# A graph-attention kernel: in its first edge walk, the two groups of a pair share one wait ahead of their sixteen gathers

## The chip, the core and the metric

The kernel runs on one core of one Trainium2 chip. The metric is the device time of one execution in microseconds (us), as the median of several runs. The core has TensorE (PE, and PEld for its weight loads), VectorE (DVE), ScalarE (ACT), GpSimd (POOL) and SyncE (SP). Each runs its own instruction stream; they meet only in semaphores. Sixteen DMA engines move data between device memory and the on-chip memory (SBUF).

## What is computed

A network of four layers on 6250 nodes and 100000 edges, 256 features a node, all in float32: graph attention with two heads and then with one, a mixture of experts, a mean over neighbours with a small dense layer, and a second mixture. The change concerns the first attention layer. Its reference, cut to what matters:

```python
def gat_layer(x, W, a_l, a_r, b, src, dst, num_nodes):
    z = (x @ W).reshape(num_nodes, heads, d)
    el = jnp.einsum('nhd,hd->nh', z, a_l)
    er = jnp.einsum('nhd,hd->nh', z, a_r)
    e = el[src] + er[dst]
    e = jnp.where(e > 0, e, NEG_SLOPE * e)
    m = jax.ops.segment_max(e, dst, num_segments=num_nodes)
    ex = jnp.exp(e - m[dst])
    s = jax.ops.segment_sum(ex, dst, num_segments=num_nodes)
    alpha = ex / s[dst]
    msg = z[src] * alpha[:, :, None]
    out = jax.ops.segment_sum(msg, dst, num_segments=num_nodes)
    return out + b[None, :, :]
```

The edges are sorted by `dst`. `src` is random, so the rows `z[src]` have to be gathered.

## The kernel before

The program is a chain of eleven phases (L2456). `walk1` is `edge_walk` with two heads (`H == 2`) and with `nodes`, an object that turns finished nodes into the next layer's rows on the side. `walk2` is the same function with one head. `walk3` is a function of its own, `mean_walk`, with its own gather (L1856).

**Tiles and groups.** A tile is 128 edges and a group eight tiles (1024 edges); there are 98 groups. A group's edges end in a window of 80 consecutive nodes. Two groups make a pair, so the walk has 49 pairs; `Z` holds the gathered rows of four pairs, one buffer `Z[k // 2]` a pair, each for sixteen tiles. The loops are unrolled over eight groups (`UNROLL`), `s` is the number of a group and `k` its place among eight.

**Gathers (L578).** POOL's whole stream is `gather(s, k)`, group after group. It waits for `done8`, which TensorE raises when a group's products are done (`done8` starts at 8, so `s + 1` means that group s-8, the last user of this half of the buffer, is through), and for `idx_ready`, which ScalarE raises when it has copied the group's indices (L596). Then it issues eight indirect DMAs, one for each tile (L583), 128 rows of 1048 bytes each.

**ScalarE** turns logits to weights (`exps`, L606), scales the second head's rows (`scale`, L614), and after a group's products runs `window` (L627): wait for `done8`, copy the next indices into `idx[k]`, copy the window out of PSUM (L633), store it. The order of a pair is: `exps`, two times `scale`, the side work's `head` (L381), `window` of the even group, the side work's `copy_out` (L389), `window` of the odd group.

**TensorE (L736, `pair`)** multiplies one-hot tiles with the gathered rows, in quarters of two tiles a group, and puts the small steps of the attention scores for two pairs ahead between the quarters: `turn_el` (L693, the first that needs the gathered rows; it waits for all sixteen gathers of that pair), `turn_ends` (L699, L700), `turn_ins` (L705, L706) ahead of the odd group's second quarter, and `columns` (L711, L712) behind the odd group. The last tile of a group waits for the window copied before it (L724), whose last node it carries over (L727).

**VectorE (L892, `pair`)** answers each of these steps: logits (L847), one-hot tiles (L803), scans of the turned scores (L817), `carries` (L828) which wait for L700, picks and sums of the target scores (L810, L812), `scan_maxima` (L837) which waits for L706, and then the side work's `scale` (L434).

**SyncE** loads the target scores and resets of three pairs ahead (L538 to L543), and loads and stores the side work's rows (L362, L367).

What orders the work is each engine's written order and these semaphores; nothing else plans it. The lines quoted here are the two waits at stake:

```python
pool.wait_ge(done8, s + 1)
pool.wait_ge(idx_ready, s + 1)
```

Of the kernel before, what the change touches and what calls it, by code (L numbers as in the profile page):

```python
# [446 lines left out]
def edge_walk(nc, keep, dram, name, table, heads, nodes=None):  # L447
# [3 lines left out]
    H = heads  # L451
# [7 lines left out]
    with Phase(nc, name) as ph:  # L459
# [58 lines left out]
        def turns(eng):  # L518
            return eng.value_load(keep["n0tab"][0:1, STEP_TAB:STEP_TAB + 1], min_val=LOOPS, max_val=LONG_LOOPS)
# [56 lines left out]
        @block.gpsimd  # L576
        def _(pool):
            def gather(s, k):  # L578
                pool.wait_ge(done8, s + 1)
                pool.wait_ge(idx_ready, s + 1)  # L580
                pool.sem_inc(pool_tick, 1)
                for t in range(GROUP_TILES):
                    pool.indirect_dma_start(  # L583
                        out=Z[k // 2][:, k % 2 * GROUP_TILES + t, :], out_offset=None, in_=table,
                        in_offset=bass.IndirectOffsetOnAxis(ap=idx[k][:, t:t + 1], axis=0)).then_inc(gathered[k], 16)
            n = turns(pool)
            gather(0, 0)
            gather(1, 1)
            with pool.Fori(0, n) as i:
                for j in range(UNROLL):  # L590
                    gather(i * UNROLL + (j + 2), (j + 2) % UNROLL)
# [1967 lines left out]
```

## Time and profile before

| | |
|---|---|
| median of 3 runs | 5288.94 us (5286.85 to 5299.87) |
| the profiled execution | 5308.62 us, its span 5306.6 us |
| PE busy | 3058.9 us (58%) |
| DVE busy | 1986.9 us (37%) |
| ACT busy | 1502.5 us (28%) |
| POOL busy | 2681.1 us (51%) |
| granted TensorE clock, mean | 0.749 of full speed |
| gathers of the first walk, L583 | 784, from 215.1 to 1475.4 us, median 953 ns |
| gathers of the second walk, L583 | 784, from 1574.8 to 2768.3 us, median 953 ns |

A span is counted from the first to the last instruction. A time on POOL is that of issuing a gather; its data lands later. "Idle before" is the time for which an engine did nothing ahead of an instruction, and "<-" names what ended it: "issue" means that nothing seen in the profile did, "remote" that a semaphore was raised at that time by something that the profile can't match with the end of an instruction. The ends of matmuls are modelled from their starts. Index copies alternate in the first walk: the first of a pair is that of its even group.

### The profile page before, as it was taken

What the parts mean: (1) busy time and instruction counts of PE and PEld (TensorE: products, weight loads), DVE (VectorE), ACT (ScalarE), POOL (GpSimd) and SP (SyncE); (2) the same over time, 40 slices, a digit from 0 to 9 for tenths busy, and PEclk for the clock granted to TensorE, in tenths of its full rate; (3) what the DMA queues carried; (4) which work ended last, traced back from release to release, by engine and by line L of the source; (5) the groups of instructions that cost most, each with busy time, mean ns of one, the idle gap of its engine ahead of it and who ended that gap; (6) DMA issues with size and microseconds to landing.
All of it is one profiled execution on the core that took longest, in us unless ns stands there. A gap on an engine that the chain in (4) does not pass through costs nothing. (4 is left out here: it accounts for less than half of the span.)

```text
span 5306.6 us, 61698 instructions
## 1 busy us (share of the span) xinstructions
PE 3058.9 (58%) x11768; PEld 1883.0 (35%) x11768; DVE 1986.9 (37%) x5614; ACT 1502.5 (28%) x4807; POOL 2681.1 (51%) x2732
## 2 busy tenths in 40 slices
PE   3245555555543455554554489921566666666699
PEld 2123333332321222222223478820333333333466
DVE  4246555555533333333336812242222222223222
ACT  2122232332221222222221023311334444444233
POOL 1366666666626666666652145525566666661121
PEclk9667767777766767677775699965777777777799
DMA  6346666666623433333334266675444444442111
GB/s 151 82 97 104 107 106 109 107 108 104 104 52 96 98 95 99 97 97 98 95 90 135 64 200 220 225 226 153 108 123 120 122 119 122 120 122 65 63 55 51
DMA packets 381422, 598.24 MB, mean 113 GB/s; under 512 B 102442, under 2 KB 272078, under 8 KB 380658
## 3 DMA queue, kind: packets, MB, share of 16 engines
q0 software_dynamic: 136000, 386.29, 32.0%
q1 hardware_dynamic: 209138, 172.22, 12.0%
q10 hardware_dynamic: 36160, 38.56, 2.4%
q14 instruction: 104, 0.85, 0.1%
q8 instruction: 20, 0.33, 0.0%
HBM read 489.46 MB, written 107.34 MB: 112 GB/s over the span
## 5 line engine op out<-in xcount | busy, mean ns | idle before, releaser
L583 POOL DMA_INDIRECT walk_rows<-z_two_heads,walk_idx x784 | 794.7, 1014 | 536.3 <-ACT walk_idx L596 302.5
L583 POOL DMA_INDIRECT walk_rows<-z_one_head,walk_idx x784 | 758.3, 967 | 534.6 <-ACT walk_idx L596 301.9
L1861 POOL DMA_INDIRECT walk_rows<-h,walk_idx x784 | 747.5, 953 | 460.6 <-issue 232.8
L2006 PE MATMUL walk_ps_part<-walk_rows,walk_whot 128*80 128x257 f32 x1568 | 538.3, 479 | 244.1 <-issue 138.2
L730 PE MATMUL walk_ps_part<-walk_rows,walk_hot 128*80 128x258 f32 x1568 | 527.4, 469 | 0.6
L730 PE MATMUL walk_ps_part<-walk_rows,walk_whot 128*80 128x257 f32 x1568 | 519.0, 478 | 0.0
L2006 PEld LDWEIGHTS walk_ps_part<-walk_rows,walk_whot 128*80 128x80 f32 x1568 | 266.5, 186 | 441.4 <-issue 405.9
L596 ACT ACTIVATE walk_idx<-keep_src 128x8 int32 x212 | 44.1, 208 | 1293.5 <-remote 952.1
L730 PEld LDWEIGHTS walk_ps_part<-walk_rows,walk_whot 128*80 128x80 f32 x1568 | 267.9, 186 | 175.9 <-issue 127.1
L730 PEld LDWEIGHTS walk_ps_part<-walk_rows,walk_hot 128*80 128x80 f32 x1568 | 254.7, 180 | 132.2 <-issue 72.8
L812 DVE TENSOR_REDUCE walk_er<-walk_picked 128x8 f32<-128x640 f32 x294 | 241.0, 820 | 29.4 <-issue 7.6
L810 DVE TENSOR_TENSOR walk_picked<-walk_hot,walk_erB 128x640 f32<-128x640 f32 x294 | 241.0, 820 | 22.0 <-issue 3.1
L705 PE MATMUL walk_ps_row_scores<-walk_ones,walk_ends 1*32 1x1 f32 (+1 forms) x196 | 20.4, 171 | 384.2 <-DVEq L832 219.2
L624 ACT ACTIVATE walk_rows<-walk_rows,walk_w 128x129 f32<-128x129 f32 x784 | 235.3, 389 | 5.8
L699 PE MATMUL walk_ps_row_scores<-keep_ident,walk_fmax 32*1 32x32 f32 (+1 forms) x98 | 18.5, 188 | 369.6 <-issue 239.2
L1585 PE MATMUL exp_ps_hid<-exp_hT,exp_w 128*128 128x256 f32 x864 | 220.2, 388 | 8.3 <-DMA exp_b<-in_ffn_b 5.7
L1577 PE MATMUL exp_ps_y<-exp_w,exp_g 128*128 128x256 f32 x864 | 222.6, 380 | 0.0
L2120 DVE TENSOR_TENSOR walk_n_y<-walk_n_h,walk_ps_n_rows 128x256 f32<-128x256 f32 x52 | 21.9, 421 | 522.1 <-DMA walk_n_agg<-agg 459.0
L621 ACT ACTIVATE walk_whot<-walk_hot,walk_w 128x80 f32<-128x80 f32 x784 | 202.9, 347 | 20.5 <-issue 12.8
L1887 ACT ACTIVATE walk_whot<-walk_hot,walk_weight 128x80 f32<-128x80 f32 x784 | 206.8, 349 | 0.0
L828 DVE TENSOR_TENSOR_SCAN walk_ends<-walk_rr,walk_ends,walk_ps_row_scores 1x16 f32<-1x16 f32 x147 | 32.9, 224 | 453.1 <-remote 387.4
L1529 POOL DMA_INDIRECT y_tokens<-exp_y,exp_home x108 | 106.1, 982 | 183.1 <-DVE exp_y L1617 166.6
(368 smaller groups left out, 5189.3 us busy)
## 6 DMA issues: line engine op xcount, KB each, us to landing
exp_w<-in_ffn_W SPq DMA_DIRECT2D x108, 512.0 KB
agg<-walk_window ACTq DMA_DIRECT2D x198, 80.3 KB
walk_rows<-z_two_heads,walk_idx POOLq DMA_INDIRECT x784
walk_rows<-z_one_head,walk_idx POOLq DMA_INDIRECT x784
comb_ya<-y_tokens POOLq DMA_DIRECT2D x28, 448.0 KB
walk_rows<-h,walk_idx POOLq DMA_INDIRECT x784
walk_erB<-er_two_heads SPq DMA_DIRECT2D x104, 80.0 KB
agg<-walk_window ACTq DMA_DIRECT2D x99, 80.6 KB
```

Of the source, the lines that this page charges most:

```text
L583: pool.indirect_dma_start(out=Z[k // 2][:, k % 2 * GROUP_TILES + t, :], out_offset=None, in_=table, in_offset=bass.IndirectOffsetOnAxis(ap ...
L621: last = act.activation(S[k % HOTS][:, t, :], S0[k % HOTS][:, t, :], ACT.Copy, scale=w[:, 0, col:col + 1])
L624: last = act.activation(row, row, ACT.Copy, scale=w[:, 1, col:col + 1])
L730: last = pe.matmul(P[k % 2][0:WIN, 0:AW].rearrange("p (h w) -> p h w", w=HW), hot[:, t, :], rows, start=t == 0, stop=t == GROUP_TILES - 1)
L810: dve.tensor_tensor(picked[:, :, :], S0[k % HOTS][:, :, :], erB[q][:, j, :, h].unsqueeze(1).to_broadcast(wide), ALU.mult)
L812: dve.tensor_reduce(er[:, h, j * GROUP_TILES:(j + 1) * GROUP_TILES], picked[:, :, :], axis=AX.X, op=ALU.add)
L1529: pool.indirect_dma_start(out=dram["ys"], out_offset=bass.IndirectOffsetOnAxis(ap=home[k][:, t:t + 1], axis=0), in_=y[k][:, t, :], in_offs ...
L1577: last = pe.matmul(psY[k][t][:, 0:D], g[k][:, hc, t * 128:(t + 1) * 128], W2[k][:, hc, :], start=hc == 0, stop=hc == HC - 1)
L1585: last = pe.matmul(psH[hc % 2][:, 0:BLOCK], W1[k][:, hf, hc * 128:(hc + 1) * 128], hT[k][:, hf, :], start=hf == 0, stop=hf == HALVES - 1)
L1861: pool.indirect_dma_start(out=Z[k // 2][:, k % 2 * GROUP_TILES + t, :], out_offset=None, in_=table, in_offset=bass.IndirectOffsetOnAxis(ap ...
L1887: last = act.activation(S[k % HOTS][:, t, :], S0[k % HOTS][:, t, :], ACT.Copy, scale=weight[k][:, t:t + 1])
L2006: last = pe.matmul(P[k % 2][0:WIN, 0:HW], S[k % HOTS][:, t, :], Z[k // 2][:, k % 2 * GROUP_TILES + t, :], start=t == 0, stop=t == GROUP_TI ...
```

## The change

For one head nothing changes. For two heads the waits ahead of an odd group's gathers go, and those ahead of an even group's ask for one more: the products of both groups of the pair that used the buffer before, and both lists of indices. The sixteen gathers are then issued in a row.

```diff
         def _(pool):
             def gather(s, k):
-                pool.wait_ge(done8, s + 1)
-                pool.wait_ge(idx_ready, s + 1)
+                if H == 1:
+                    pool.wait_ge(done8, s + 1)
+                    pool.wait_ge(idx_ready, s + 1)
+                elif k % 2 == 0:
+                    pool.wait_ge(done8, s + 2)
+                    pool.wait_ge(idx_ready, s + 2)
                 pool.sem_inc(pool_tick, 1)
                 for t in range(GROUP_TILES):
                     pool.indirect_dma_start(
```

## Rows read from the trace of the kernel before

**Rows 1.** Busy us (and counts) by stretch: PE, PEld, DVE, ACT, POOL, PEclk, DMA share, GB/s

```profile
322.00:1462.00 1140.00, 647.72 (x2465) 359.22 (x2464) 655.29 (x1584) 334.90 (x1234) 713.40 (x704) 0.72 0.63 107
...
3727.00:4804.00 1077.00, 703.07 (x2404) 392.56 (x2405) 264.72 (x880) 452.56 (x1460) 679.33 (x712) 0.75 0.45 121
```

**Rows 2.** The line of the index copies, L596, from 322 to 1462 us

```profile
L596 ACT ACTIVATE walk_idx<-keep_src x89: 208/208/210, 322.7 to 1460.9; 128x8 int32 x89
```

**Rows 3.** The list of waits, 322 to 1462: us in total, times, longest us

```profile
POOL walk_rows L583 <- ACT walk_idx L596: 216.6, 53, 8.3
POOL walk_rows L583 <- issue: 209.1, 647, 4.8
...
DVE walk_gkc L837 <- remote: 226.1, 16, 17.1
...
DVE walk_ends L828 <- remote: 34.1, 7, 8.1
```

**Rows 4.** Timeline, first walk: start, us, engine, line, operation, count [idle <-releaser]

```profile
802.56 0.20 PE L706 MATMUL walk_ps_row_scores<-walk_ones,walk_begins 1*32 1x1 f32 x2
...
805.55 0.66 PE L730 MATMUL walk_ps_part<-walk_rows,walk_hot 128*80 128x258 f32 x2
...
815.14 0.15 DVE L837 COPY walk_gkc<-walk_ps_row_scores 32x2 f32<-32x2 f32 x1 [12.17 <-remote]
...
815.40 0.21 ACT L596 ACTIVATE walk_idx<-keep_src 128x8 int32 x1 [9.78 <-remote]
```

**Rows 5.** Timeline of POOL's gathers, first walk, 792 to 832 us

```profile
792.28 0.95 POOL L583 DMA_INDIRECT walk_rows<-z_two_heads,walk_idx  x1 [2.59 <-ACT walk_idx L596]
...
803.21 0.95 POOL L583 DMA_INDIRECT walk_rows<-z_two_heads,walk_idx  x1 [0.30 <-issue]
...
812.00 0.95 POOL L583 DMA_INDIRECT walk_rows<-z_two_heads,walk_idx  x1 [0.30 <-issue]
816.40 0.95 POOL L583 DMA_INDIRECT walk_rows<-z_two_heads,walk_idx  x1 [3.45 <-ACT walk_idx L596]
...
831.61 1.23 POOL L583 DMA_INDIRECT walk_rows<-z_two_heads,walk_idx  x1 [5.37 <-ACT walk_idx L596]
```

**Rows 6.** Timeline of a long run of gathers, first walk, 986 to 1003 us

```profile
986.01 1.33 POOL L583 DMA_INDIRECT walk_rows<-z_two_heads,walk_idx  x1 [4.70 <-ACT walk_idx L596]
...
1000.44 0.23 DVE L828 TENSOR_TENSOR_SCAN walk_ends<-walk_rr,walk_ends,walk_ps_row_scores 1x16 f32<-1x16 f32 x1
...
1002.36 0.21 ACT L596 ACTIVATE walk_idx<-keep_src 128x8 int32 x1 [1.78 <-issue]
```

**Rows 7.** Timeline after POOL's start at 816.40: TensorE, and ScalarE's index copy

```profile
819.04 0.42 PE L693 MATMUL walk_ps_row_scores<-keep_ident,walk_rows 128*32 128x128 f32 x1
...
827.14 0.23 PE L700 MATMUL walk_ps_row_scores<-keep_ident,walk_bmax 32*1 32x32 f32 x1
...
832.88 0.20 PE L706 MATMUL walk_ps_row_scores<-walk_ones,walk_begins 1*32 1x1 f32 x2
...
835.88 0.66 PE L730 MATMUL walk_ps_part<-walk_rows,walk_hot 128*80 128x258 f32 x2
...
830.61 0.21 ACT L596 ACTIVATE walk_idx<-keep_src 128x8 int32 x1 [1.90 <-PE walk_ps_part L730]
```

**Rows 8.** Timeline of the walk's start: the sixteenth gather, and the first transpose

```profile
234.07 0.95 POOL L583 DMA_INDIRECT walk_rows<-z_two_heads,walk_idx  x1 [0.30 <-issue]
...
236.98 0.37 PE L693 MATMUL walk_ps_row_scores<-keep_ident,walk_rows 128*32 128x128 f32 x1 [71.39 <-DMA walk_rows<-z_two_heads,walk_idx]
```

**Rows 9.** Timeline of POOL in the third walk: first gathers of two runs

```profile
4031.36 0.94 POOL L1861 DMA_INDIRECT walk_rows<-h,walk_idx  x1 [4.22 <-ACT walk_idx L1874]
...
4055.43 0.94 POOL L1861 DMA_INDIRECT walk_rows<-h,walk_idx  x1 [4.21 <-ACT walk_idx L1874]
```

**Rows 10.** Timeline of the first walk's end: last gather, and pair 45's second index copy

```profile
1475.43 0.95 POOL L583 DMA_INDIRECT walk_rows<-z_two_heads,walk_idx  x1 [0.30 <-issue]
...
1480.99 0.21 ACT L596 ACTIVATE walk_idx<-keep_src 128x8 int32 x1 [0.95 <-issue]
```

## The prediction

> **What bounds it now.** I read the busy time by stretch first [rows 1]. From 322 to 1462 us, the steady part of the first walk, 704 gathers run, sixteen for each of 44 pairs, in 1140 us: 25.91 us a pair. POOL is busy for 713.40 us, the largest figure of any engine, yet only 63% of the stretch; TensorE has 647.72 and VectorE 655.29. No engine is full. The index copies give the same period: the second copy of pair 0 at 322.7 and that of pair 44 at 1460.9 are 1138.2 us, or 25.87 us a pair, apart [rows 2].
>
> The list of waits says what lies between the gathers [rows 3]. POOL waits 209.1 us for "issue", the 0.30 us between two gathers, and 216.6 us for `walk_idx`, that is for ScalarE's copy. A pair on POOL is thus 713.40/44 = 16.21 us of gathers, 4.75 us of gaps and 216.6/44 = 4.92 us of waits for indices; together 25.88. The last of the three is the only one that the change touches. The other two make a floor of 20.96 us.
>
> Why is ScalarE late? Look at the timeline of one pair [rows 4]. TensorE's L706 (which announces `ins_turned`) ends at 802.76, but VectorE, which waits for it at L837 and nothing else, starts at 815.14 after 12.17 us idle. The second group's last product ends at 806.21; ScalarE copies the indices at 815.40. Two announcements of TensorE, 3.5 us apart, thus reach their readers 0.3 us apart. POOL's rows stand beside them [rows 5]: its run of sixteen gathers goes from 792.28 to 812.95 and the readers wake 2.2 to 2.5 us after it. So I read: **while POOL issues gathers, TensorE's announcements can be held, and they come free some 2.3 us after POOL falls silent**. In this walk VectorE lost 226.1 us at L837 so, 16 times, and 34.1 us at L828, 7 times [rows 3].
>
> A different row shows that this is not always so. In the run from 986.01 the scan L828, which waits for L700's `ends_turned`, starts at 1000.44 with no idle time before it, and the first group's index copy comes at 1002.36, 16 us into the run [rows 6]. A hold catches some announcements, and those behind it.
>
> **The change, part by part.** The `H == 1` branch is the old code, so the second walk stands, and the third has its own function. In the first walk:
> - The waits of odd k go. Inside a run the next group's first gather (803.21, the ninth from 792.28) follows after the same 0.30 us as any other [rows 5], so the waits cost nothing where they are met, and their going gives nothing: term 0.
> - The waits of even k move to both products and both copies. The first group's eight gathers now start with the second index copy rather than with the first. At pair 20 they start at 831.61, 1.0 us after the first copy at 830.61; they would start 1.0 us after the second, as the gathers at 816.40 follow the copy at 815.40. The eight gathers of the odd group follow them, and so end later by eight gathers, 10 us.
> - Nothing but gathers stands on POOL's queue behind the wait; SyncE's and ScalarE's own DMAs are not moved past anything in program order. The indices of the first group simply lie ready longer.
>
> **Cover of the later gathers.** Pair p+4's gathers start with the end of pair p and are first needed at the transpose of pair p+2 (L693). After a second copy at 815.40 that transpose comes at 819.04 [rows 7], so need lies one period and 2.6 us after the burst's start: 27 us at a period of 24.4. The burst takes 15 x 1.257 + 0.95 = 19.8 us, up to 20.7 as in [rows 5]; landing takes 1.9 us more, by the first sixteen (last issued at 234.07, ends 235.02, transpose at 236.98) [rows 8]. 22.6 against 27: covered by 4 us. If that cover were gone, each us would cost 44.
>
> Here the Trainium skill speaks against the change: "DMA: Bandwidth & Descriptors", Rules for kernel authors, says to issue a DMA early and wait for it late. The change issues half of them late. By that rule alone it gains nothing and, where cover runs out, loses; the rows above say that cover holds.
>
> **The new pair.** After a burst that began at a second copy, TensorE's steps are in the rows already [rows 7], counted from POOL's start at 816.40: L700 (`ends_turned`) ends at 10.97, the first group's index copy comes at 14.2, L706 ends at 16.7, the second group's last product at 20.1. Now the burst has sixteen gathers, so all of these fall into it. If the first two pass and the rest are held, all is flushed at the burst's end, 20.0 to 20.9 us, and POOL starts 3.45 us after its end, as at 816.40 [rows 5]. L837 then runs at the flush again, as at 815.14, so the pattern repeats. One wait a pair: 16.21 + 4.75 + 3.45 = **24.41 us** against 25.88, 1.47 less, times 44 = 64.7 us saved. The run 792.28 to 816.40 is such a period already: 24.12. The third walk, whose POOL code is the old one but which runs in bursts of sixteen by itself, shows 24.07 from 4031.36 to 4055.43, with 4.21 idle [rows 9]; with 4.21 the saving is 31 us.
>
> **The end of the walk** gives a little back. The last burst ended 15.4 us after pair 44's second copy (1460.9 to 1476.38) and pair 45's copy followed at 1480.99, 20.1 us after [rows 10]. New: 1.0 to the start, 20.7 of burst, 2.4 to the flush: 24.1, so 4.0 us lost. Sum: -64.7 + 4.0 = -61 us. The profiled execution took 5308.62 us, 0.37% over the median of 5288.94; the sum gives 5248 against it and **5228 us** against the median, which I forecast. The ends of this term: 24.07 a pair gives -76 (5213), 4.21 idle gives -27 (5262).
>
> **Rivals.** (A) *First group's announcement held as well*, on and off. A hold at 13.6 us stops the window copy (L633), on which the second group's last tile waits. After the flush come 0.6 us of copies, 1.3 of TensorE (an estimate: the last tile's 0.66 [rows 7] and as much for the carry product ahead of it), then 1.2 to POOL: period 20.9 + 2.3 + 3.1 = 26.3, that is 0.4 x 44 + 4 = +22, 5311 if at every pair, 5270 if at half. For: the burst will lie over it, where the eight gathers from 816.40 had ended before it. Against: at 1002.36 it passed deep in a run. 14%.
>
> (B) *Slower: the hold catches `ends_turned`.* Place: L700 at 10.97 of each burst. It decides if L828 waits at most pairs. TensorE then cannot reach the second group's last three quarters: after the flush VectorE's carries take 1.0 (an estimate: four scans of L828's 0.23 [rows 6]), and L706 to the last product 3.5 (832.88 to 836.54 [rows 7]), with 1.2 to POOL: 20.9 + 2.3 + 4.7 + 1.2 = 29.1, or with a burst of 20.7, 28.9. That is +3.0 x 44 + 4 = +136: 5425; at a quarter of the pairs with the rest as forecast, 5278. For: the burst reaches over it for the first time; L828 was held 7 times. Against: 7 of 44 only, and it passed at 1000.44. 20%.
>
> (C) *Nothing changes.* The idle time only moves from before the odd group to before the even one, so that waits a pair stay 4.92: 5289 to 5293. The Trainium skill would have it so: "TensorE: Matmul & The Clock Gate", The cost: per-tile semaphore tail, counts some 26 ns for an increment on a matmul, and with no holds POOL's quiet has nothing to free. The trace disagrees (12 us at L837), so 8%.
>
> Forecast 58%.
>
> **Numbers.** 0.3% (16 us) is about what a measurement of this kernel can tell from no change. Faster: forecast, plus part of A and B's mild form, 0.64. Same: C and the middle of A, 0.14. Slower: 0.22. The range starts below the -76 end at 5205 and reaches over A at 5311 to 5325, leaving most of B out.
>
> **To check in the new trace.** Runs of sixteen on POOL throughout the walk, each after 3.4 to 4.2 us idle; the period by index copies near 24.4; POOL's wait for `walk_idx` near 44 rather than 53 times and 150 us rather than 216.6; TensorE's L693 not waiting for a gather; the second walk unchanged. Wrong if L828 waits about 10 us at most pairs (B), if POOL's idle stays at 4.9 (C), or if L693 waits for a DMA.

## The result, and the profile after

The changed kernel took 5334.24 us (median of 10 runs, 5310.56 to 5347.6) where the kernel before took 5295.1 (10 runs) beside it: ratio 1.0065, 95% interval 1.0047 to 1.0083. It is slower, by 0.65%; the forecast of 5228 us was wrong. The profiled execution took 5336.71 us, 28.1 more than that of before. Lines behind L578 have moved by 4 (L596 is L600 now, L837 is L841).

The busy time by stretch, the first walk's steady part and the third walk's:

```profile
322.00:1462.00 1140.00, 697.39 (x2400) 372.04 (x2401) 633.47 (x1534) 325.92 (x1194) 682.43 (x685) 0.70 0.59 104
3727.00:4804.00 1077.00, 680.94 (x2328) 380.83 (x2327) 258.89 (x860) 443.22 (x1427) 672.02 (x706) 0.75 0.45 119
```

Against [rows 1] 685 gathers fit into the stretch and no longer 704. TensorE's granted clock is 0.70, not 0.72; it has more busy time and fewer instructions. The index copies, from pair 0's second to pair 44's:

```profile
L600 ACT ACTIVATE walk_idx<-keep_src x89: 208/208/211, 315.9 to 1487.2; 128x8 int32 x89
```

They are 1171.3 us apart, 44 pairs, 26.62 a pair against 25.87 [rows 2]. So the balance is: pair 0 done 6.8 us earlier (315.9 against 322.7), 44 pairs 33.1 us longer, and the walk's end, from pair 44's copy to pair 45's at 1511.9, 24.7 against 20.1 [rows 10], 4.6 longer. That is +30.9, and the second walk's first gather starts at 1605.58, 30.8 after before's 1574.82. What follows gives some of it back, with unchanged code: the second walk's last gather starts 25.3 us after before's (2793.6 against 2768.3), the third walk's first 27.6 (3653.2 against 3625.6). The whole loss is in the first walk.

The list of waits, 322 to 1462 us (us in total, times, longest):

```profile
ACT walk_idx L600 <- remote: 320.2, 42, 14.8
DVE walk_gkc L841 <- remote: 274.0, 38, 11.1
POOL walk_rows L587 <- ACT walk_idx L600: 241.0, 41, 14.5
POOL walk_rows L587 <- issue: 216.2, 644, 6.9
...
DVE walk_ends L832 <- remote: 14.3, 2, 8.6
...
PE walk_ps_row_scores L697 <- DMA walk_rows<-z_two_heads,walk_idx: 10.1, 8, 3.8
```

Against [rows 3] POOL waits for indices fewer times (41, not 53) but longer (241.0 us, not 216.6), where 150 was forecast. L828's successor L832 was held twice: rival B did not come. L697 hardly waits for a gather: the cover held. What grew is L841's wait, 38 times instead of 16. The list of before has one row more that the prediction did not use, the wait of the index copies themselves:

```profile
ACT walk_idx L596 <- remote: 365.7, 37, 13.6
```

Its total is no smaller than the 320.2 us of after; what changed is which group's copy waits. Of the copies of pairs 1 to 44 in before, the first group's waited for a remote step 3 times, all the others were the second group's. In after the first group's waited so 31 times.

Three runs of sixteen gathers follow, by POOL's timeline (all other gathers between these rows have 0.30 us before them):

```profile
638.48 0.95 POOL L587 DMA_INDIRECT walk_rows<-z_two_heads,walk_idx  x1 [4.69 <-ACT walk_idx L600]
...
657.87 0.95 POOL L587 DMA_INDIRECT walk_rows<-z_two_heads,walk_idx  x1 [0.30 <-issue]
665.96 0.95 POOL L587 DMA_INDIRECT walk_rows<-z_two_heads,walk_idx  x1 [7.14 <-ACT walk_idx L600]
...
690.18 0.95 POOL L587 DMA_INDIRECT walk_rows<-z_two_heads,walk_idx  x1 [3.83 <-ACT walk_idx L600]
...
717.90 0.95 POOL L587 DMA_INDIRECT walk_rows<-z_two_heads,walk_idx  x1 [7.65 <-ACT walk_idx L600]
```

and ScalarE's index copies, first and second group of each pair:

```profile
661.69 0.21 ACT L600 ACTIVATE walk_idx<-keep_src 128x8 int32 x1 [11.38 <-remote]
...
664.95 0.21 ACT L600 ACTIVATE walk_idx<-keep_src 128x8 int32 x1 [0.95 <-issue]
...
676.81 0.21 ACT L600 ACTIVATE walk_idx<-keep_src 128x8 int32 x1 [2.03 <-PE walk_ps_part L734]
...
689.18 0.21 ACT L600 ACTIVATE walk_idx<-keep_src 128x8 int32 x1 [1.30 <-remote]
```

The second pair (start 665.96) comes nearest to the forecast's: the first group's copy passes 10.9 us into the run, the second comes 2.8 us after the run's end (686.36), POOL starts again after 3.83 us, and the period is 24.22 us, where 24.41 was forecast. The first pair (638.48) is rival A: nothing reaches ScalarE until 661.69, 2.9 us after the run's end. Its period is 27.48, and that of the third pair (690.18), held as well, 27.72 (to the next start at 717.90). TensorE's timeline says that the first group's products had long been done:

```profile
648.65 0.18 PE L704 MATMUL walk_ps_row_scores<-keep_ident,walk_bmax 32*1 32x32 f32 x1
...
650.76 1.15 PE L734 MATMUL walk_ps_part<-walk_rows,walk_hot 128*80 128x258 f32 x2
...
673.11 0.23 PE L704 MATMUL walk_ps_row_scores<-keep_ident,walk_bmax 32*1 32x32 f32 x1
...
675.30 1.15 PE L734 MATMUL walk_ps_part<-walk_rows,walk_hot 128*80 128x258 f32 x2
```

The last product ends at 651.91, 13.4 us into its run, and is read 9.8 us later; in the next run it ends at 676.45, 10.5 us in, and is read 0.4 us later. Sorted over the walk by whether ScalarE's first copy comes before or after the end of POOL's run, 24 pairs pass with a mean of 25.4 us and 20 are held with a mean of 28.1; (24 x 25.4 + 20 x 28.1)/44 = 26.6. "Pass" is not "on time": at 11 of the 24 the copy waited 3.7 to 9.7 us for a remote step and then came inside the run.

The two kinds often alternate. In the rows above, TensorE's steps have caught up after the held pair before the next run starts, so the next pair's steps come early in the run (L704 ends 7.4 us in) and pass. After the passed pair, L716 is done only behind the start (690.99 against 690.18), L704 ends 10.4 us in, and the announcement is held again. Over the walk this is a tendency and no rule: where L704 ends less than 9 us into the run, 1 of 12 pairs is held, elsewhere 19 of 32; a held pair follows a held one 7 times.

### The profile page after: what moved, and what is told of

Read it like the earlier page. It is cut to its first block and busy times, and to the rows that moved or that the text cites. A ratio compares the mean times of both kernels' runs of the same rounds, so it can differ in the third digit from the quotient of the medians.

```text
span 5334.8 us, 61650 instructions
## 1 busy us (share of the span) xinstructions
PE 3155.4 (59%) x11768; PEld 1921.4 (36%) x11768; DVE 1981.8 (37%) x5614; ACT 1504.5 (28%) x4807; POOL 2673.0 (50%) x2732
## 5 line engine op out<-in xcount | busy, mean ns | idle before, releaser
L587 POOL DMA_INDIRECT walk_rows<-z_two_heads,walk_idx x784 | 780.6, 996 | 579.1 <-ACT walk_idx L600 332.9
L2010 PE MATMUL walk_ps_part<-walk_rows,walk_whot 128*80 128x257 f32 x1568 | 532.2, 475 | 218.2 <-issue 117.4
L734 PE MATMUL walk_ps_part<-walk_rows,walk_hot 128*80 128x258 f32 x1568 | 573.8, 502 | 0.9 <-issue 0.4
L734 PE MATMUL walk_ps_part<-walk_rows,walk_whot 128*80 128x257 f32 x1568 | 539.2, 492 | 1.5 <-issue 1.2
L600 ACT ACTIVATE walk_idx<-keep_src 128x8 int32 x212 | 44.1, 208 | 1224.4 <-remote 982.7
L734 PEld LDWEIGHTS walk_ps_part<-walk_rows,walk_hot 128*80 128x80 f32 x1568 | 277.3, 195 | 147.2 <-issue 97.7
L715 PE MATMUL walk_ps_cols<-walk_ends,walk_ones 1*128 1x4 f32 (+1 forms) x196 | 47.5, 310 | 367.5 <-DVEq L847 209.1
L814 DVE TENSOR_TENSOR walk_picked<-walk_hot,walk_erB 128x640 f32<-128x640 f32 x294 | 241.1, 820 | 31.4 <-issue 14.2
L841 DVE COPY walk_gkc<-walk_ps_row_scores 32x2 f32<-32x2 f32 (+1 forms) x98 | 14.5, 148 | 614.0 <-remote 541.1
L2124 DVE TENSOR_TENSOR walk_n_y<-walk_n_h,walk_ps_n_rows 128x256 f32<-128x256 f32 x52 | 21.9, 421 | 524.4 <-DMA walk_n_agg<-agg 409.0
```

Of the source, the lines that this page charges most:

```text
L587: pool.indirect_dma_start(out=Z[k // 2][:, k % 2 * GROUP_TILES + t, :], out_offset=None, in_=table, in_offset=bass.IndirectOffsetOnAxis(ap ...
L734: last = pe.matmul(P[k % 2][0:WIN, 0:AW].rearrange("p (h w) -> p h w", w=HW), hot[:, t, :], rows, start=t == 0, stop=t == GROUP_TILES - 1)
L814: dve.tensor_tensor(picked[:, :, :], S0[k % HOTS][:, :, :], erB[q][:, j, :, h].unsqueeze(1).to_broadcast(wide), ALU.mult)
L2010: last = pe.matmul(P[k % 2][0:WIN, 0:HW], S[k % HOTS][:, t, :], Z[k // 2][:, k % 2 * GROUP_TILES + t, :], start=t == 0, stop=t == GROUP_TI ...
```

## The experiments

Five batches, each with the kernel before beside it; runs of one batch are compared only within it. The code below is cut to the edit; `...` marks what is left out. What the kernel before took matters: 5302.88, 5259.63 and 5256.03 us in the first three, 4666.18 and 4664.2 in the last two.

**The first group's announcement made earlier** (on the changed kernel and on before):

```
                 products(s, 2 * m, 2)
+                if H == 2:
+                    products(s, 2 * m, 3)
                 if turn is not None:
                     turn_ends(p + 2)
-                products(s, 2 * m, 3)
+                if H == 1:
+                    products(s, 2 * m, 3)
```

> The changed kernel, with the even group's last quarter of products put ahead of turn_ends on TensorE (first walk only), so that its done8 comes some 5 us earlier in POOL's run of sixteen. Theory H (TensorE's announcements are held while POOL issues; the even group's at 13.6 us into the run is what the change lost): it passes at most pairs, POOL's idle time falls from 5.9 to 3.5-4 us, the pair from 26.6 to 24.4-25 us, the kernel from 5334 to 5240-5265. Rival L (the loss is that half of the gathers start 10 us later, whatever the order on TensorE): 5334, pair 26.6.

> The kernel before with the same edit on TensorE alone. Theory H: the even group's indices are copied earlier, the two runs of eight merge into one of sixteen more often, pair 24.4-25.4 us, kernel 5230-5275. Rival L: no difference, 5295.

`q3_after` took 5351.67 us, 1.0107 of before (1.0089 to 1.0125): slower, where 5240 to 5265 was expected. `q3_before` took 5281.92, 0.9959 (0.9944 to 0.9974): a gain, just short of the expected one. The waits of `q3_after`, 322 to 1462 us:

```profile
POOL walk_rows L587 <- ACT walk_idx L600: 261.5, 43, 11.0
...
DVE walk_ends L835 <- remote: 157.9, 20, 11.6
DVE walk_gkc L844 <- remote: 152.4, 32, 10.3
ACT walk_idx L600 <- remote: 133.1, 24, 11.6
```

The index copy is held much less (133.1 us against 320.2), as wanted, but `ends_turned`, which now comes after it, is held in its place: 157.9 us against 14.3. With the order of the two announcements turned round, the hold went from one to the other, so it isn't bound to one of them.

**Less to gather.** `half_after` issues four of a group's eight gathers in the first walk (the other tiles are zeros); `narrow_after` issues all, each with 131 of a row's 262 numbers (the others are zeros).

```
# half_after (LOADED is 4 with two heads)
-                for t in range(GROUP_TILES):
+                for t in range(LOADED):
# narrow_after (ROW is 131 with two heads)
-                        out=Z[...][:, ..., :], ..., in_=table,
+                        out=Z[...][:, ..., 0:ROW], ..., in_=table.rearrange("n (h w) -> (n h) w", w=ROW),
```

> The changed kernel with four of a group's eight gathers in the first walk (the other rows of the buffer are zeroed once; every other instruction stays). Theory H: POOL's run is 10 us, nearly all announcements fall behind it, and the pair takes what TensorE and VectorE need of each other, 19.5-21 us: kernel 5050-5110. Rival C (the engines' own chain needs 26 us a pair and POOL is a bystander): 5320-5340.

> The changed kernel with all sixteen gathers of a pair but half the bytes in each (131 of 262 elements a row, first walk only; the other half of the buffer is zeroed once). Theory H with POOL's issuing as the cause of the holds: period stays 26-27 us, kernel 5320-5340. Rival D (the traffic of the gathers on the DMA engines holds the announcements): holds shrink, period 20-24 us, kernel 5060-5220.

`half_after` took 4925.6 us (before 5302.88), less than the 5050 to 5110 expected, and `narrow_after` 5329.76, as expected if POOL's issuing is the cause. Each ran once. `narrow_after`'s waits are those of the changed kernel:

```profile
ACT walk_idx L603 <- remote: 315.5, 37, 14.8
DVE walk_gkc L847 <- remote: 267.9, 39, 11.0
```

Half the bytes a gather change nothing. Half the instructions change much. The first walk of `half_after` ends before 1200 us, so its stretch is 322 to 1100 us, which holds 84 index copies:

```profile
ACT walk_idx L603 <- remote: 43.2, 12, 4.4
```

The changed kernel's L600 waits 211.0 us, 28 times, in the same stretch, and the old L841, which waits 180.9 us there, does not wait for a remote step at all. Both kernels move about half the bytes; only the one that issues half the gathers, in runs of eight, loses most of the holds. The holds go with POOL's issuing, not with the traffic that it starts.

**SyncE's part.** While announcements are held, some of SyncE's steps are slow too. A row SPq is one of them. The step that issues L368's DMA takes 0.70 us in the held run above, and about as long at the median of the stretch (ns: shortest, median, longest):

```profile
643.52 0.70 SPq L368 DMA_DIRECT2D er_one_head<-walk_n_z  x1
...
L368 SPq DMA_DIRECT2D er_one_head<-walk_n_z x42: 4/699/728, 347.3 to 1456.1; - x42
```

So a theory S was tried: SyncE's steps beside the gathers hold the announcements. First its six loads of a pair in the first walk were given to ScalarE (`act_*`, behind its second window copy), left out (`quiet_*`), or made to wait until POOL had issued a run's last gather (`gate_*`):

```
# quiet (with two heads)
-                    load(p + AHEAD, (m + AHEAD) % INS)
+                        sp.wait_ge(inputs_used4, p + (AHEAD + 1))
+                        sp.sem_inc(inputs[(m + AHEAD) % INS], LOADS)
# gate: POOL raises `silent` behind each odd group's gathers
+                    if H == 2:
+                        sp.wait_ge(silent, p + 3)
+                        ...
                     load(p + AHEAD, (m + AHEAD) % INS)
```

> The changed kernel, with the six loads of a pair (target scores and resets of four pairs ahead) issued by ScalarE behind its second window instead of by SyncE, in the first walk. Theory S (in a run of gathers each of SyncE's steps takes 0.7 us instead of 0.04, and while it steps so, TensorE's announcements are held; a SyncE that waits holds none): with some 40 steps fewer a pair the even group's announcement passes, POOL's idle time falls to 3.5-4 us, the pair to 24-25 us and the kernel to 5220-5270. Rival P (POOL's issuing alone holds TensorE, whoever else is at work): 5320-5350, and more if ScalarE's own steps slow down.

> The kernel before with the same move of the loads from SyncE to ScalarE. Theory S: L837's holds (226 us in the steady part) shrink by more than half and the kernel is 5150-5250. Rival P: 5280-5310.

> The changed kernel with SyncE's six loads of a pair left out of the first walk's loop (the scores and resets of the first four pairs are used again and again; SyncE only raises the semaphore). Theory S: as act_after or a little faster, 5200-5260. Rival P: 5320-5340.

> The changed kernel, with SyncE's six loads of a pair held back until POOL has issued the last gather of a run, so that most of SyncE's steps fall into POOL's silence. Theory S (TensorE's announcements are held while SyncE steps at 0.7 us a step beside the gathers): most holds in the run go, the first group's index copy passes at two pairs in three or more, period 24.5 to 25.5, time 0.975 to 0.990 of before. Rival P (POOL's issuing alone holds them, SyncE is a bystander): holds stay as they are, 1.003 to 1.010. The node loads and stores of SyncE are not gated, so part of the holds can stay under S as well.

> The same gate on the kernel before. Theory S: fewer of the 12 us waits at L837, period 24.6 to 25.4, time 0.980 to 0.993 of before. Rival P: 0.998 to 1.003.

> The kernel before with the gate and with the last quarter of the first group's products ahead of the transposes of the ends. If the two gains add, 0.976 to 0.989 of before under theory S; under rival P the quarter's gain alone, 0.994 to 0.998.

`act_after` took 5358.07 us, 1.0201 of before (1.0181 to 1.022), `act_before` 5461.05, 1.0397 (1.0364 to 1.043); both are far above theory S's range, and the first is what rival P allows if ScalarE's steps slow down. No index copy waited for a remote step in either, but in `act_after` the old L841 still did (141.2 us, 29 times). ScalarE, behind its DMAs, was late for its own work: its first step of a pair's weights (`exps`) waited, for nothing that another engine did,

```profile
ACT walk_ps_work L614 <- issue: 365.5, 42, 15.8
```

against 94.3 us in the changed kernel, and 487.2 us in `act_before`. POOL stood still longer with it (670 gathers in the stretch, and 629), so these runs can't say whether the copies were on time because SyncE had fewer steps or because the pairs were stretched.

`quiet_after` can say it in part: SyncE has the same steps left in it, and ScalarE none more. It took 5247.37 us in its one run, 0.998 of before's 5259.63, which is in theory S's range, but its waits are not what theory S needs:

```profile
DVE walk_gkc L845 <- remote: 336.9, 44, 9.9
ACT walk_idx L604 <- remote: 265.2, 45, 10.9
```

The loads gone, the holds are still there. At 10 pairs of 44, instead of 20, the first group's copy came only after the run's end, and a pair took 25.3 us in the mean. So SyncE's loads are not what holds announcements, though they may lengthen a hold.

`gate_after` took 1.0072 of before (1.0057 to 1.0087), `gate_before` 1.0004 (0.9992 to 1.0015), `gate_q3_before` 0.9966 (0.9951 to 0.9981). All three are in rival P's ranges, and the gated kernel's index copies are held as long as before:

```profile
ACT walk_idx L608 <- remote: 307.9, 43, 14.3
```

But the gate did not do what it was meant to. By the traces 170 of the 255 load DMAs of SyncE start inside POOL's runs in the changed kernel, and 165 of 264 in `gate_after`; before has 165 of 264, and `gate_before` 185 of 270. Hardly a step was moved into silence, so these runs test neither theory. The quarter's gain of `q3_before` came again (0.9966 beside 0.9959).

**The run split in two**, so that the announcement falls into silence:

```
                 elif k % 2 == 0:
                     pool.wait_ge(done8, s + 2)
                     pool.wait_ge(idx_ready, s + 2)
+                else:
+                    pool.wait_ge(done8, s + 2)
```

> The changed kernel with one more wait: an odd group's gathers also wait for the first products of the next pair. Eight gathers start with a pair, then POOL is silent until the first group's announcement is in, then the other eight follow: the same gathers, the odd ones later still. Theory A (the loss comes from the first group's announcement, due 13.6 us into a run of sixteen, being held): it falls into silence here, so its index copy comes at about 14 to 15 us after POOL's start at nearly every pair, and the loss goes: period 25.2 to 26.1, time 0.985 to 1.000 of before. Rival, the late gathers cost by themselves (transposes or scans wait for them): later gathers cost more, the time is 1.007 or above of before and L697 waits for a gather.

5258.51 us, 1.0003 of before (0.9992 to 1.0014): the loss of the change alone (1.0065 in its own batch) is gone, but not in the way expected, as the waits show:

```profile
PE walk_ps_row_scores L699 <- DMA walk_rows<-z_two_heads,walk_idx: 419.9, 37, 15.2
...
POOL walk_rows L589 <- PE walk_ps_part L736: 164.1, 48, 6.5
...
DVE walk_ends L834 <- remote: 100.4, 25, 5.1
...
ACT walk_idx L602 <- remote: 78.1, 15, 9.5
```

The holds at the index copy shrank (78.1 us against 320.2) and so did all at the old L841; in their place TensorE's transposes wait 419.9 us for gathers, which now come half a pair later still. The odd gathers run together with the next even ones, in runs of sixteen again. Both effects, less hold and less cover, lie in this run, and it prices neither. The time lies between the two ranges.

**The hold's price alone.** In the changed kernel the second group's last tile waits for the first group's window copy, and ScalarE's second index copy comes behind both. `loose_*` cuts that; what a first group carries into the second is left out.

```
-                        pe.wait_ge(win_ready2, s + 2)
+                        alone = H == 2 and k % 2 == 1
+                        if not alone:
+                            pe.wait_ge(win_ready2, s + 2)
                         ...
-                            pe.matmul(..., wsb[1 - k % 2][:, cols], ...)
+                            pe.matmul(..., (nil if alone else wsb[1 - k % 2])[:, cols], ...)
# ScalarE, behind an even group's window copy; the odd group's own wait and index copy go
+                if H == 2 and k % 2 == 0:
+                    act.wait_ge(done8, s + (UNROLL + 2))
+                    copy_idx(second, k + 1)
```

> In the changed kernel the held announcement of the first group costs because the second group's last tile (by the carry product) and ScalarE's second index copy queue up behind it. Here the second group's carry product reads a tile of zeros instead of the first group's window and does not wait for it, and ScalarE copies the second group's indices straight behind the first window copy. What a first group carries into the second is left out, so those rows of the output differ. Theory A: holds stay where they are but cost nothing, the second index copy comes under 1 us behind the first after a run's end, the period is 24.2 to 25.2 at every pair, 0.98 to 0.99 of the kernel before, and the gap to loose_before is gone (0.985 to 1.000). Rival (late gathers, or something else that the change brings): the period stays near 26 and the gap to loose_before stays at 1.005 or more.

> The same edit on the kernel before. Its holds fall on L706's announcement, which this edit does not touch, so it gains what ScalarE's earlier second copy gives, some 1 us at pairs without a hold: 0.985 to 0.998 of before.

> The changed kernel of quiet_after again, timed: SyncE's six loads of a pair are left out and their semaphore is raised at once (pairs then use the input values that the first loads brought, so the output differs). If the loads themselves (their steps, or their transfers) hold announcements in the changed kernel above all, this is 0.990 to 1.000 of the kernel before, and the gap to quiet_before is under 1.003. If they are a bystander, the gap stays at 1.005 or more.

> The same edit on the kernel before: SyncE's six loads of a pair left out. By either theory 0.985 to 1.000 of the kernel before.

Here the ground moved. The kernel before, unchanged, took 4666.18 us (33 runs), 11 to 12% less than in the batches so far, and the four others the same within 0.2%: `loose_after` 1.0016 (1.0007 to 1.0025), `loose_before` 0.9999 (0.999 to 1.0008), `quiet_after3` 1.0002 (0.9993 to 1.0012), `quiet_before` 0.9993 (0.9983 to 1.0002). The expectations for holds could not be tested, because there were next to none (one wait of 2.1 us in `loose_after`, none in the two `quiet` kernels). The same two kernels ran once more, with the changed kernel itself.

> The changed kernel itself, beside the kernel before and the two loose kernels. Where TensorE's announcements are held during runs of gathers (before near 5260 to 5300 us): 1.004 to 1.009 of before by theory A. Where none is held (before near 4666 us, POOL issuing without a pause in the first walk): no hold to price, only the later gathers are left, 1.000 to 1.004.

> loose_after once more, since its first runs fell where nothing was held. Where announcements are held again, theory A: the second index copy comes under 1 us behind the first after a run's end, period 24.2 to 25.2, 0.98 to 0.99 of before and no gap to loose_before (0.985 to 1.000). Rival: period near 26, a gap of 1.005 or more. Where nothing is held: 1.001 to 1.003, as the first time.

> loose_before once more. Where announcements are held: 0.985 to 0.998 of before. Where nothing is held: 0.999 to 1.001.

Again before took 4664.2 us (29 runs). **The changed kernel took 4667.19: 1.0005 (0.9996 to 1.0015)**, no difference. `loose_after2` took 1.0018 (1.0008 to 1.0029), `loose_before2` 1.0002 (0.9991 to 1.0013). All three are in their ranges for the case without holds. Both times `loose_after` was 0.2% slower than before and `loose_before` was not; no run says why. The changed kernel's waits there, 322 to 1262 us (43 pairs):

```profile
PE walk_ps_row_scores L697 <- DMA walk_rows<-z_two_heads,walk_idx: 386.3, 43, 11.6
ACT walk_idx L600 <- PE walk_ps_part L734: 262.5, 86, 3.8
POOL walk_rows L587 <- issue: 199.1, 648, 1.1
...
POOL walk_rows L587 <- ACT walk_idx L600: 12.3, 33, 1.3
```

No line waits for a remote step; every index copy follows its product; POOL waits 12.3 us for indices where it waited 241.0, and 688 gathers fit into 940 us, which is 21.9 us a pair. POOL hardly pauses, TensorE waits 9 us a pair for it, and it makes no difference which group's indices a run begins with. Each of the 86 index copies in the stretch starts 0.12 to 0.14 us after the modelled end of its product, and with nothing held there is nothing for the change to free, as the prediction had it in its rival C. The Trainium skill ("TensorE: Matmul & The Clock Gate", The cost: per-tile semaphore tail) counts some 26 ns for the increment. These rows, with 0.13 us for the increment, the wait and the start together, leave room for that figure and can't show it by itself. SyncE's step, beside an unbroken run of gathers, takes half of what it took with holds:

```profile
L368 SPq DMA_DIRECT2D er_one_head<-walk_n_z x50: 332/344/362, 335.4 to 1355.6; - x50
```

## Why the prediction was wrong

**What bounds the kernel**: right. Where nothing is held, nearly all of POOL's 4.92 us a pair for indices is gone (12.3 us at 43 pairs, 0.3 us each), and a pair takes 21.9 us.

**The waits of odd k, term 0**: right; the ninth gather of a run follows after 0.30 us. **The cover**: right for the changed kernel (L697 waited 10.1 us in 8 waits), and `split_after` shows what it costs where it is gone. **The end of the walk**, +4.0: it was +4.6. That pair 0 came 6.8 us earlier was not in the sum.

**The step that failed** is "If the first two pass and the rest are held", which put L700's and the first group's announcements 10.97 and 13.6 us into a run (the copy at 14.2), both passing. L700's did. The first group's did not: at 20 of 44 pairs ScalarE read it only after POOL's run had ended, and at 11 more it was 3.7 to 9.7 us late inside the run. That is rival A, "on and off", which had 14%. The one wait of 3.45 us a pair, and so the 24.41, rested on this step; 26.6 us a pair came of it.

The evidence taken for it was a copy that passed 16 us into a run at 1002.36 [rows 6]. A count over all of before would not have warned either: in its runs of 24 gathers the first group's copy came 16.3 to 18.4 us into the run six times with no remote wait, and was held twice, 22.5 us in or later. How deep an announcement lies in a run thus doesn't decide by itself. What does is not known. The place that the forecast needed, 13 to 14 us into a run of sixteen, was empty in before: its first group's copies came 8.4 to 8.7 us into such a run, or in POOL's silence.

**Rival A's price** was too low as well: 26.3 a pair was forecast and 27.48 and 27.72 are what the rows show. The term is the 3.1 us from flush (the moment when the held announcements are read) to POOL's start. It took 4.3 (661.69 to 665.96): TensorE's last tile is done at 663.42, but ScalarE's second copy comes at 664.95, behind a window DMA, two node copies and 0.95 us of its own register steps. With 28.1 at held pairs and 25.4 at the others, 20 and 24 of them, the 64.7 us saved become 33.1 lost.

**The saving where it passes** was half luck. The pair from 665.96 took 24.22, near the forecast 24.41, but with a run 0.6 us shorter and a wait 0.4 longer than in the sum, and its copy came 10.9 us in because the pair before had been held. The four pairs whose copy came near the forecast place without a remote wait (13.4 to 14.3 us in) took 25.0 to 25.8, 25.3 in the mean. So the term for a pair without a hold, 1.47 us saved, was too large too: about 0.6.

In rival B, L706 to the last product is 3.66 us by its own rows (832.88 to 836.54) and not 3.5; its sum uses the right one.

**What is shown and what is not.** The rows show the loss being made: copy late, second copy late behind it, POOL late. With holds the loss of 0.65% is there, without them the same two kernels differ by 0.0005, with an interval that leaves the loss out. That is a contrast between two conditions, not an edit, and more than the holds differs between them: without holds POOL hardly waits for an index at all, and the granted clock in the first walk is 0.78 against 0.70 (0.72 in before). So a cost that only shows where POOL waits, or one through the clock, is not excluded. The edit that was to take the hold's price away (`loose_*`) never ran where there were holds, and stays open. So does what opens and closes a hold. POOL's issuing is needed for it (`half_after`, `narrow_after`); SyncE's loads are not (`quiet_after`); whether its other steps, slowed in the same stretches, take part or only suffer was not settled.

`q3_before`, before with the first group's last quarter ahead of L700, was faster than both kernels where there are holds (0.9959, and with the gate 0.9966). It was not run where there are none.

## What to carry to other kernels

Before a wait is moved so that a burst grows longer, list every announcement that falls into the burst and price the case that each is late, with the queue of the engine that reads it, not only the one wait that goes. Count over all pairs, and by announcement: the total of one line was about the same in both kernels here, and it was another group that waited. A row in which something passed is evidence for the pattern that it lies in, not for one that the change makes. Before an experiment's time is read, look in its trace whether the edit moved what it was to move. And if a gain rests on idle time whose releaser is "remote", find out first whether that time is there each time the kernel runs.

## What the runs showed of the hardware

The kernel before, unchanged, took 5256 to 5303 us in three batches and 4664 to 4666 in two. One of the chips showed both (5302.88, and 4666.18 later). In the one condition, TensorE's announcements can reach other engines some 10 us late while POOL issues gathers (651.91 to 661.69 above), and the step of SyncE that issues L368's DMA takes 0.70 us at the median; in the other, the index copy follows the product at each of 92 copies and the same step takes 0.33 to 0.36. Not every step differs: L543's takes some 0.69 us in both. Most gathers take 0.95 us with 0.30 between in both. What sets the condition is not known; a ratio of a per cent or less between such kernels holds for one condition only.

In this kernel the increment that a TensorE instruction makes is thus not always seen when the instruction ends. In another one with long runs of indirect DMAs the waits named "remote" are the place to look for it.
